# A four-batch selective-scan and mixture-of-experts kernel on one Trainium2 core: the last batch's routing is reordered, and ten expert-weight pieces are loaded inside its scan

## The reference

```python
xn = _layernorm(x)                       # [2048, 512]
scores = softmax(xn @ gate_w.T)          # 64 experts
topk_w, topk_i = top_k(scores, 6)
# each token takes a place in each of its experts, in token order, at most 64 places per expert
y = (silu(buf @ w_gate) * (buf @ w_up)) @ w_down      # one 64-row buffer per expert
out = x + sum over k of y[expert, place] * topk_w + shared_expert(xn)
```

## Time and profile before

| | us |
|---|---|
| median of 3 runs | 1035.92 (1034.25 to 1036.40) |
| the profiled execution, own time | 1035.54 |
| its span, first to last instruction | 1033.8 |
| TensorE busy / weight loads | 860.1 / 477.7 |
| VectorE, ScalarE, GpSimd busy | 601.4, 500.3, 565.3 |
| HBM read and written | 230.67 MB and 19.17 MB, 242 GB/s over the span |

### The profile page before, as it was taken

One profiled execution on the slowest core, in us unless ns is written; L12 is line 12 of the kernel. 1 busy time (PEld: TensorE's weight loads), 2 busy tenths in 40 slices (PEclk: granted clock), 3 DMA queues, 4 the chain that ended last, 5 costly groups with the idle time before them and its releaser, 6 DMA issues.

```text
span 1033.8 us, 12606 instructions
## 1 busy us (share of the span) xinstructions
PE 860.1 (83%) x4223; PEld 477.7 (46%) x4223; DVE 601.4 (58%) x859; ACT 500.3 (48%) x899; POOL 565.3 (55%) x318
## 2 busy tenths in 40 slices
PE   6376656667999787999789968999999987999984
PEld 3154544455554464555555453444444443444431
DVE  4589899889888988998798733212222211111111
ACT  4589545797766788766755233222222211221110
POOL 0387998987988988979787601122222222112121
PEclk9568655688999998999899969999999999999998
DMA  8633344335334543343546377999999999999995
GB/s 281 233 122 123 125 163 142 124 121 166 127 122 143 196 163 98 123 122 123 203 126 238 124 295 270 381 390 386 398 398 390 393 397 398 396 386 399 387 386 143
DMA packets 68412, 250.67 MB, mean 242 GB/s; under 512 B 10506, under 2 KB 13078, under 8 KB 68092
## 3 DMA queue, kind: packets, MB, share of 16 engines
q1 hardware_dynamic: 54740, 226.09, 58.0%
q0 software_dynamic: 7712, 18.88, 7.5%
q10 hardware_dynamic: 5896, 4.90, 1.4%
HBM read 230.67 MB, written 19.17 MB: 242 GB/s over the span
## 4 chain that ended last, share of the span: by engine, by line
PE 49%; DVE 16%; DMA 12%; issue 6%; ACT 6%; SPq 3%; POOL 1%; POOLq 0%; DVEq 0%; ACTq 0%
PE ps L672 11%; PE ps L868 10%; DMA arena<-in_L_ffn_w_down 9%; PE ps L667 9%; PE ps L683 8%; PE ps L892 6%; DVE ps L1254 6%; DVE arena L1261 4%; SPq L562 3%; DVE arena L1280 2%; ACT ps L1063 2%; DVE arena L1254 1%; PE ps L901 1%; PE ps L780 1%; DMA xn_rows<-scores 1%
## 5 line engine op out<-in xcount | busy, mean ns | idle before, releaser
L1490 POOL TENSOR_TENSOR arena<-arena 128x1024 f32<-128x1024 f32 x128 | 300.0, 2361 | 57.4 <-DMA arena<-bc_rows 39.5
L667 PE MATMUL ps<-ident,arena 128*128 128x128 f32 (+2 forms) x1408 | 238.2, 321 | 84.6 <-DVE ps L1262 39.7
L667 PEld LDWEIGHTS ps<-ident,arena 128*128 128x128 f32 (+2 forms) x1408 | 199.3, 177 | 189.3 <-issue 84.4
L1063 ACT ACTIVATE ps<-arena,An 128x511 f32<-128x511 f32 x256 | 165.2, 680 | 109.2 <-DVE ps L1262 93.4
L1254 DVE TENSOR_TENSOR_SCAN ps<-ps,arena 128x1024 f32<-128x1024 f32 x82 | 187.6, 2288 | 15.5 <-ACT ps L1063 14.7
L868 PE MATMUL ps<-arena 128*64 128x352 f32 x984 | 161.8, 467 | 10.2 <-issue 6.5
L672 PE MATMUL ps<-xnT,sw 128*128 128x512 f32 x320 | 152.5, 621 | 12.7 <-ACT arena L1024 11.8
L1504 POOL DMA_INDIRECT arena<-xn_rows,idu x32 | 34.0, 1064 | 212.4 <-DVE wcol L1400 165.8
L1495 POOL TENSOR_TENSOR arena<-arena 128x1024 f32<-128x1024 f32 x46 | 108.3, 2355 | 49.6 <-DVE arena L1254 45.2
L1407 DVE TENSOR_TENSOR arena<-arena,ps 128x352 f32<-128x352 f32 x32 | 16.7, 522 | 175.3 <-PE ps L868 175.3
L868 PEld LDWEIGHTS ps<-arena 128*64 128x64 f32 x984 | 74.3, 138 | 84.9 <-issue 74.3
(11 more groups left out here) (165 smaller groups left out, 914.2 us busy)
## 6 DMA issues: line engine op xcount, KB each, us to landing
arena<-bc_rows SPq DMA_DIRECT2D x128, 512.0 KB, 4.7
arena<-in_L_ffn_w_down SPq DMA_DIRECT2D x59, 768.0 KB, 23.0
arena<-in_L_ffn_w_gate SPq DMA_DIRECT2D x64, 704.0 KB, 23.8
arena<-in_L_ffn_w_up SPq DMA_DIRECT2D x59, 704.0 KB, 23.6
arena<-in_x SPq DMA_DIRECT2D x4, 1024.0 KB, 6.9
xn_rows<-xn ACTq DMA_DIRECT2D x4, 1024.0 KB, 5.8
out_rows<-arena SPq DMA_DIRECT2D x4, 1024.0 KB, 5.2
extra<-in_L_ffn_w_up SPq DMA_DIRECT2D x5, 704.0 KB, 22.5
```

What stands on the lines that cost most here:

```text
L667: return nc.tensor.matmul(dst, src, ident[0:k, 0:k], is_transpose=True, **kw)
L1063: a = nc.scalar.activation(ps[:, 2 * (c % 2) + n, 1:L], dt[k][:, 1:L], ACT.Exp, scale=An[:, k, NB * g + n:NB * g + n + 1])
L1490: G.tensor_tensor(R[c % RING], dtu[k][:, None, :].to_broadcast([P, NB, L]), Brep[n % REPS], ALU.mult)\
```

## The change

It touches the last batch, and the places in the arena.

- `score`, `norm` and `sc_store` of the last batch are due right behind each other (41.45 to 41.65 instead of up to 42.47), ahead of the first `scopy` (42.29).
- The copies of the transposed rows of the last batch (`xnT`) are done by VectorE instead of ScalarE.
- `pos` is split in two. `pospre` (due 41.2, behind the last logits and ahead of the first `sgate`) puts in the constants, the expert's number and the sums of earlier batches; `pos` adds what depends on the mask. Both use one matmul over several quarters at once. In other batches both parts run as one job. `msum` of the last batch, which nobody reads, is left out.
- A new TensorE job `warm` (due 37.0, ahead of the first `xnT`) does 44 transpositions of the identity into PSUM bank 3.
- Ten pieces instead of seven are due at t - 13 + n; piece 10 at t - 0.4; pieces 11 to 19 at t + 2.3; piece 20 at t + 8. For this, `dt` and `dtu` are laid out by halves, so that the memory of the scan's first half comes free early, the `xb` buffers rotate, so that the first of them is batch 1's, and the order of `slots` changes. The waits of the pieces change with it.

```diff
+TAILFILL = 44
@@ LAST
-    "act score": [40.79, 41.22, 41.46, 41.47],
+    "act score": [41.45, 41.46, 41.47, 41.48],
-    "act norm": [42.39],
-    "act sc_store": [42.47],
+    "act norm": [41.6],
+    "act sc_store": [41.65],
+    "pe warm": [37.0],
+    "pe pospre": [41.2],
@@ LASTBANKS
+    "warm": [3],
+    "pospre": [2],
@@ build
-        dt = [carve(L) for _ in range(DC)]
-        dtu = [carve(L) for _ in range(DC)]
+        halves = [[carve(L) for _ in range(4)] for _ in range(2)]
+        dt = halves[0][0:2] + halves[1][0:2]
+        dtu = halves[0][2:4] + halves[1][2:4]
...
+        xb = [xb[2], xb[0], xb[1]]
...
-        slots += [arena[:, n * SLOT:(n + 1) * SLOT] for n in range(6, ASLOTS)]
+        slots += [arena[:, n * SLOT:(n + 1) * SLOT] for n in [ASLOTS - 2] + list(range(6, ASLOTS - 2)) + [ASLOTS - 1]]
...
+                        if job == "act xnT" and b == B - 1:
+                            engine = "dve"
...
-            for n in range(7):
+            for n in range(10):
                 add(t - 13 + n, "sp", "piece", 0, n)
-            for n in range(7, 10):
-                add(t - 0.4 + 0.01 * n, "sp", "piece", 0, n)
             for n in range(10, SLOTS):
-                add(t + (2.3 if n < SLOTS - 2 else 8.0) + 0.01 * n, "sp", "piece", 0, n)
+                add(t + (-0.4 if n == 10 else 2.3 if n < SLOTS - 1 else 8.0) + 0.01 * n, "sp", "piece", 0, n)
@@ sync
                     elif c == 7:
+                        sp.wait_ge(s["out_st"], 16 * (B - 2))
+                    elif c == 8:
+                        sp.wait_ge(s["dA_done"], NQ - STEPS // 2)
+                        sp.wait_ge(s["dbu_done"], NQ - STEPS // 2)
+                    elif c == 10:
                         sp.wait_ge(s["dA_done"], NQ)
                         sp.wait_ge(s["dbu_done"], NQ)
-                    elif c == 10:
+                    elif c == 11:
                         sp.wait_ge(s["yT_mm"], NQ)
-                    elif c == 13:
+                    elif c == 18:
                         sp.wait_ge(s["g_ready"], NC)
-                    elif c == SLOTS - 2:
+                    elif c == SLOTS - 1:
                         sp.wait_ge(s["out_st"], 16 * B)
-                        sp.wait_ge(s["xn_ready"], NC)
@@ tensor
+                elif kind == "warm":
+                    claim(bank)
+                    for n in range(TAILFILL):
+                        transpose(ps[:, bank, 0:P], ident[:], start=True, stop=True)
...
-                elif kind == "pos":
-                    claim(bank)
...
+                elif kind in ("pospre", "pos"):
+                    counts = ps[:, bank, 0:LT * E].rearrange("p (t e) -> p t e", t=LT)
+                    if kind == "pospre" or b < B - 1:
+                        claim(bank)
+                        if b == 0:
+                            pe.wait_ge(s["const"], 2)
+                        nc.tensor.matmul(ps[:, bank, LT * E:(LT + 2) * E], ident[:], iot[:], start=True, stop=True)
+                        nc.tensor.matmul(counts, ones[0:1, :], iota_b[0:1, None, :].to_broadcast([1, LT, E]),
+                                         start=True, stop=False)
                         for k in range(b):
-                            nc.tensor.matmul(dst, ones[:], msum[k][:], start=False, stop=False)
...
+                            nc.tensor.matmul(counts, ones[:], msum[k][:, None, :].to_broadcast([P, LT, E]),
+                                             start=False, stop=False)
+                    if kind == "pos":
+                        pe.wait_ge(s["mask_ready"], b + 1)
+                        for k in range(LT - 1):
+                            nc.tensor.matmul(counts[:, k + 1:LT, :], ones[:],
+                                             mask[:, k, None, :].to_broadcast([P, LT - 1 - k, E]), start=False, stop=False)
+                        nc.tensor.matmul(counts, ltri[:], mask[:], start=False, stop=True).then_inc(s["pos_mm"], 1)
+                        freed[bank] = [(s["ohe_ready"], b + 1)]
@@ vector
+                elif kind == "xnT":
+                    dve.wait_ge(s["xnT_mm"], i + 1)
...
+                    V.tensor_copy(xnT[:, :, c * P:(c + 1) * P],
+                                  ps[:, BANK["xnT", b, c], :].rearrange("p (c t) -> p c t", c=HC)).then_inc(s["xnT_ready"], 1)
...
+                    if b < B - 1:
                         with nc.allow_low_precision("sums of one-hot rows, exact"):
                             V.tensor_reduce(msum[b][:], mask[:].rearrange("p t e -> p e t"), AX_X, ALU.add)
```

More of the change, by code:

```diff
@@ L783, in _ @@
                     freed[bank] = [(s["ex_done"], LT * (b + 1)), (s["mask_ready"], b + 1)]
-                elif kind == "pos":
-                    claim(bank)
-                    if b == 0:
-                        pe.wait_ge(s["const"], 2)
-                    pe.wait_ge(s["mask_ready"], b + 1)
-                    for t in range(LT):
-                        dst = ps[:, bank, t * E:(t + 1) * E]
-                        nc.tensor.matmul(dst, ltri[:], mask[:, t, :], start=True, stop=False)
-                        for k in range(t):
-                            nc.tensor.matmul(dst, ones[:], mask[:, k, :], start=False, stop=False)
-                        for k in range(b):
-                            nc.tensor.matmul(dst, ones[:], msum[k][:], start=False, stop=False)
-                        nc.tensor.matmul(dst, ones[0:1, :], iota_b[0:1, :], start=False, stop=True)
-                    nc.tensor.matmul(ps[:, bank, LT * E:(LT + 2) * E], ident[:], iot[:], start=True, stop=True)\
-                        .then_inc(s["pos_mm"], 1)
-                    freed[bank] = [(s["ohe_ready"], b + 1)]
+                elif kind in ("pospre", "pos"):
[7 more added lines that the diff above has]
+                                         start=True, stop=False)
+                        for k in range(b):
+                            nc.tensor.matmul(counts, ones[:], msum[k][:, None, :].to_broadcast([P, LT, E]),
[7 more added lines that the diff above has]
+                        freed[bank] = [(s["ohe_ready"], b + 1)]
@@ L1312, in _ @@
                     V.bn_stats(zstats[:, c, :], xb[p][:, c, :]).then_inc(s["zst_ready"], 1)
+                elif kind == "xnT":
+                    dve.wait_ge(s["xnT_mm"], i + 1)
+                    dve.wait_ge(s["lg_mm"], LT * b)
+                    dve.wait_ge(s["su_mm"], NI * b)
+                    dve.wait_ge(s["sg_mm"], NI * b)
+                    V.tensor_copy(xnT[:, :, c * P:(c + 1) * P],
+                                  ps[:, BANK["xnT", b, c], :].rearrange("p (c t) -> p c t", c=HC)).then_inc(s["xnT_ready"], 1)
                 elif kind == "xstats":
@@ L1351, in _ @@
                         a = V.max(p8[:, t, :], zz[:, t, :])
-                    with nc.allow_low_precision("sums of one-hot rows, exact"):
-                        V.tensor_reduce(msum[b][:], mask[:].rearrange("p t e -> p e t"), AX_X, ALU.add)
+                    if b < B - 1:
+                        with nc.allow_low_precision("sums of one-hot rows, exact"):
+                            V.tensor_reduce(msum[b][:], mask[:].rearrange("p t e -> p e t"), AX_X, ALU.add)
                     link(a)
```

## The result

The changed kernel takes 1031.70 us in the median of 20 runs (1026.52 to 1038.74), the kernel before, beside it, 1036.16 us (20 runs, 1033.09 to 1041.71). The ratio is 0.9956, with a 95% interval from 0.9939 to 0.9974: faster by 4.5 us, where 9.3 were forecast. The profiled execution of the changed kernel took 1031.32 us, its span is 1029.6 us.

The account below looks back on a forecast made before the run. The first weight refill, behind pair 0's gates, was taken to set the end. An earlier scores' store (7.65 us) and the gates' clock (1.7) gave 9.3 us, so 1026.6 us was predicted, range 1024.3 to 1033.0.

Parts of the forecast that it names:

- What bounds the kernel: Start of the second phase: the end moves one for one with the first weight refill, after pair 0's gates on TensorE.
- Rival D: Second phase: TensorE, 94% busy, binds instead of the first refill; no gain, within 2 us of 1035.9; chance 0.06.
- The warm-up: TensorE before the last batch's xnT: 44 transpositions cost 0, keep the full clock, and logits end 4.8 us earlier.
- The rest of the sum: Last batch's routing from logits through scores' store and gather to pair 0: store lands 7.65 us earlier, refill 9.3 us earlier.
- Counts and shared gate: TensorE around the mask: pospre 1.0 us, first half-group 1.7, remaining counts 0.5, done at 613.7 us instead of 620.4.
- term of 1.7 us for the gates' clock: Pair 0's gates on TensorE: after a 0.5 us pause they run at full clock instead of 0.50, saving 1.7 us.
- Rival B: Last batch's logits on TensorE: the clock falls after the warm-up, 3.3 to 3.5 us saved, 1032.4 us; chance 0.17.
- The early pieces at 0: Weight queue before the refill: three earlier pieces empty it 5.8 us sooner, but refills start later, so 0 gain.
- The copies: Last batch's xnT copies on VectorE: 0.1 us more each, but ScalarE is freed and the rows' store goes out at 607.2.
- Rival A: Scores' store: lands only when the weight queue runs dry, at 629.4; 7.5 us saved, 1028.4 us; chance 0.15.
- Rival C: The warm-up itself: TensorE runs at the lower clock through it and the fill, 2.9 us lost, 1038.8 us; chance 0.04.

Follow-up runs that it names:

- e9: The changed kernel itself (44 transpositions), unedited and measured again: 1031.34 us, ratio 0.9951 to the kernel before.
- e1: The changed kernel with 66 transpositions in the warm-up instead of 44: 1027.66 us, ratio 0.9916 to the kernel before.
- e10: The changed kernel with 66 transpositions instead of 44, a second time with more executions: 1029.67 us, ratio 0.9928 to the kernel before.
- e11: The changed kernel with 66 transpositions and without pospre, all counts in one job: 1027.00 us in 4 runs, ratio 0.9905 to the kernel before.
- e3: The changed kernel (44 transpositions) with pieces 7 to 9 due behind the scan's end again: 1033.20 us, ratio 0.9963 to the kernel before.
- e6: The changed kernel with 66 transpositions and pieces 7 to 9 behind the scan again: 1033.28 us, ratio 0.9977 to the kernel before.

## Why the prediction was wrong, point by point

- **What bounds the kernel**: right. The first refill moves the end one for one, to within 2 us either way, in fourteen profiles; the DMA share from 650 to 1014 us is 1.02 or 1.03 in all of them. Rival D falls.
- **The warm-up: the step that failed.** I wrote: "I take the full clock, because work fills two thirds of the time from 597.6 to 604.9 where there was none". The 2.45 us pause behind the warm-up was as forecast, but the clock fell in all four profiles with 44, and in the changed kernel's the transpositions and logits took their 10.3 us at the lower clock as before. With 66 transpositions it didn't fall there in any of seven profiles. The mechanism, idleness brings the lower clock, was right; that a pause of 2.45 us behind 4.9 us of work is enough was misjudged, and that 44 can be worse than none wasn't seen. The warm-up's term was priced at 4.8 us of logits and measured 0.2 in the profile (17.8 to 17.6) and 1.4 in e9 (16.4). The refill came 3.2 us earlier in the one and 5.7 in the other, where 9.3 were forecast.
- **The rest of the sum, given the clock.** Against e1 the forecast's chain (behind a scan that ends at 597.5) is right to about 1 us everywhere: logits 13.0 forecast and 13.8 measured, fill 16.2 and 16.5, table 24.8 and 25.1, store issued 18.3 and 19.2, gathered rows 35.0 and 35.7, refill 39.6 and 40.2, time 1026.6 and 1027.7 (e10: 1029.7). Counts and shared gate cost what was written, though I had miscounted the matmuls of the old counts (24; there are 27). The term of 1.7 us for the gates' clock was paid in e1 and e11 alone among the seven profiles with 66: that the clock holds there was a second weak step, and with 44 it held in all four profiles.
- **Rival B** was the case that came: forecast 3.3 to 3.5 us, in the profile 3.2 us of refill, median 4.5. Its parts were right in that profile, TensorE's last fill binding and the gates at full clock. In e9 the clock fell too, but the store binds, and 5.7 us of refill were gained; B had taken it that the clock stays down through all of the logits. `pospre` took 1.6 us where 1.5 was written, and the table started 30.8 us behind the scan where 31.3 was written. I gave it 0.17 and the forecast 0.52.
- **The early pieces at 0**: right in the profiles of the changed kernel and e3, wrong for the case that I forecast. I compared the queue's end with the refill, and left out the gather's own data, which takes 6.8 instead of 4.1 us beside the weights; the gates' clock, lost in e6, is lost in e10 too.
- **The copies**: right that they give nothing to the logits and that the rows' store goes out earlier; what that store is worth was seen with 66 alone, as 0.9 us of refill against e10 and 3.0 against e1.
- **Rival A**: falls by e6. The store lands amid the weights.
- **Rival C**: it did not happen; the clock was full during the warm-up in every profile.

## What to carry to other kernels

A filler for TensorE's clock has to reach up to the work that it is to speed up: one that stopped 2.45 us short put the loss of the clock onto the work itself, and was some 2.7 us slower than none. And a filler that does its work need not pay: 66 transpositions kept the clock over the logits, but the reordered kernel's time with them can't be told from that without any, so the kernel without the filler has to be measured too. When a chain leads to a transfer through a queue that is otherwise full, moving bulk loads out of its way can pay even if the queue would have run dry before the end of the chain (e6). And one profile is one execution: the changed kernel's refill was at 45.7 in one and 43.2 in the other, and 66's at 40.2 and 42.3, so a step read off single profiles is known only to such a difference.

## What the hardware did that I had not expected

Once down, the granted clock stayed at 0.50 for long although TensorE's records fill the time (13.60 of 13.60 us in the changed kernel's low stretch). The Trainium skill ("TensorE: Matmul & The Clock Gate", Part 1 on the clock gate, under "What's actually happening") has activity lift the throttle; the trace agrees only in part: the transpositions and narrow logits kept it down for 6.8 us in two of the four profiles with 44 and for 13.6 us in the other two. The same work never brought it down when it started at the full clock. The stretch's length changes from execution to execution of one kernel (13.6 us in one profile of the changed kernel and 6.8 in the other), and the logits end 17.6 or 16.4 us behind the scan with it. The counts and the first half-group of the shared gate are slower with it as well, so that the fill starts at 22.2 or 19.2, 3.0 us apart. That covers the refill, which differs by 2.5 between them, since in e9 TensorE then waits for the rows; the whole spread of the times, 12 us in the changed kernel, isn't explained by it. The scan itself ends between 595.4 and 600.7 us in the fourteen profiles; what moves it wasn't examined.
